# Causal attention with dot-product and geometric logits: scores and maxima as pairs of 64-row tiles, masks in VectorE, both V blocks of a step in a row

## The reference, cut to what matters

```
q, k, v     = split(x @ qkv_w + qkv_b)                     # 16 heads x 16
dot_logits  = (q @ k.T) * 16 ** -0.5
w, r        = exterior(x_prev @ w1_write, x @ w2_write), exterior(x @ w1_read, x @ w2_read)   # 16 heads x 6, unit length
geo_logits  = (r @ (w @ J6).T) * inc_scale                 # x_prev: the token before
combined    = (1 - gate) * softmax(causal(dot_logits)) @ v + gate * softmax(causal(geo_logits)) @ geo_v
y           = layernorm(x + combined @ out_w + out_b)
out         = layernorm(y + (silu(y @ wg.T) * (y @ wu.T)) @ wd.T)
```

## Time and profile before

| | us |
|---|---|
| median of 3 runs (2104.53 to 2110.35) | 2105.75 |
| profiled execution, from its first to its last instruction | 2112.1 |
| TensorE / ScalarE / VectorE / GpSimd busy in it | 1930.6 / 1273.4 / 1129.4 / 336.9 |
| `project`, until the first score | 0 to 251 |
| `attend` | 251 to 1766 |
| `finish` | 1766 to 2112 |

### The profile page before, as it was taken

How to read it: one execution, slowest core, us unless ns; L and a number is a source line. 1 busy time by engine, 2 the same in 40 slices (tenths; PEclk the granted TensorE clock), 3 DMA queues, 4 the chain that set the end, 5 groups by cost and what they waited for, 6 DMA issues and landing times. The chain is left out here.

```text
span 2112.1 us, 35917 instructions
## 1 busy us (share of the span) xinstructions
PE 1930.6 (91%) x11400; PEld 769.0 (36%) x11400; DVE 1129.4 (53%) x2179; ACT 1273.4 (60%) x1641; POOL 336.9 (16%) x609
## 2 busy tenths in 40 slices
PE   8888498999998999999899999989999995899998
PEld 4444122333332333333233333323333322556555
DVE  5666377565564655556465655646565403443442
ACT  4555544577776777677677767767777783222121
POOL 3333303111211110111111011111101111000000
PEclk9999699999999999999999999999999997999999
DMA  6668660404133250414324041432500004112000
GB/s 192 205 211 254 163 107 25 86 21 90 37 70 46 50 86 6 91 20 73 49 47 86 6 91 21 72 46 50 86 6 30 4 11 103 43 51 65 20 20 20
DMA packets 138525, 145.83 MB, mean 69 GB/s; under 512 B 46784, under 2 KB 120768, under 8 KB 136288
## 3 DMA queue, kind: packets, MB, share of 16 engines
q1 hardware_dynamic: 137136, 140.32, 30.4%
q0 software_dynamic: 624, 2.75, 0.4%
q10 hardware_dynamic: 576, 0.28, 0.1%
HBM read 88.25 MB, written 54.53 MB: 68 GB/s over the span
## 5 line engine op out<-in xcount | busy, mean ns | idle before, releaser
L931 ACT ACTIVATE prob<-ex 128x1024 f32<-128x1024 f32 (+2 forms) x1280 | 1074.5, 893 | 444.4 <-PE ex L776 438.8
L946 DVE TENSOR_REDUCE mp<-mx 128x1 f32<-128x512 f32 (+3 forms) x1280 | 749.2, 609 | 547.4 <-PE mx L794 287.5
L776 PE MATMUL ex<-qa,ka 98*128 98x512 bf16 (+3 forms) x2560 | 675.6, 354 | 62.7 <-issue 28.3
L827 PE MATMUL pv<-prob,va 128*32 128x512 f32 (+3 forms) x5120 | 613.4, 552 | 7.6 <-POOL prob L752 7.3
L791 PE MATMUL mx<-ka,qa 96*128 96x512 bf16 (+3 forms) x1280 | 450.1, 353 | 14.7 <-DVE mp L946 13.8
L752 POOL TENSOR_SCALAR_AFFINE_SELECT prob<-prob 128x256 f32<-128x256 f32 x512 | 205.8, 408 | 1288.3 <-ACT prob L931 1287.8
L776 PEld LDWEIGHTS ex<-qa,ka 98*128 98x128 bf16 x2560 | 200.2, 99 | 474.3 <-ACT prob L931 306.3
L791 PEld LDWEIGHTS mx<-ka,qa 96*128 96x128 bf16 x1280 | 123.7, 97 | 340.4 <-DVE mp L946 239.1
L827 PEld LDWEIGHTS pv<-prob,va 128*32 128x32 f32 x5120 | 101.7, 108 | 206.7 <-issue 181.8
L1291 ACT ACTIVATE sg<-pg 128x512 f32<-128x512 f32 x48 | 28.7, 597 | 185.6 <-PE pg L1213 185.5
L794 PE MATMUL mx<-mask_qk,ident 128*128 128x128 bf16 x512 | 113.1, 221 | 0.0
(11 more groups left out here) (101 smaller groups left out, 964.7 us busy)
## 6 DMA issues: line engine op xcount, KB each, us to landing
parts<-sp SPq DMA_DIRECT2D x64, 384.0 KB, 3.3
qa<-parts SPq DMA_DIRECT2D x192, 128.0 KB, 6.7
ka<-parts SPq DMA_DIRECT2D x192, 128.0 KB, 8.6
values<-vn SPq DMA_DIRECT2D x64, 256.0 KB, 3.3
va<-values SPq DMA_DIRECT2D x16, 1024.0 KB, 13.8
heads<-on SPq DMA_DIRECT2D x64, 128.0 KB, 1.9
att<-heads SPq DMA_DIRECT2D x64, 128.0 KB, 3.0
xc<-in_xt SPq DMA_DIRECT2D x8, 513.0 KB, 4.2
```

The source lines that it names most:

```text
L776: last = pe.matmul(dst, ka[which][0:NROWM, h, kb * P:(kb + 1) * P], qa[which][0:NROWM, h, (qt + 1) * CH - w:(qt + 1) * CH], start=True, st ...
L827: last = pe.matmul(pv[h * VW:(h + 1) * VW, qt % 2, CH - w:CH], va[kind][:, kb, h * VW:(h + 1) * VW], prob[(s * HG + h) % 8][:, at[j]:at[j] ...
L931: act.activation(prob[n % 8][:, 0:w], ex[:, n % 2, 0:w], ACT.Exp).then_inc(ex_done, 1)
L946: v.tensor_reduce(out=mp[kind][:, h * NKB + qb, k0 // CH:k0 // CH + 1], in_=mx[:, u % 2, 0:w], axis=AX.X, op=ALU.max).then_inc(mx_free[kin ...
```

## The change

A unit of a step is now one block of two heads, each head's scores in one bank of the slot: units 0 and 1 are the first block, 2 and 3 the second. For GEO, 6 components in 6 products and 2 maxima rows are 38 rows; the two heads of a unit stand on partitions 0 to 37 and 64 to 101. A DOT score matmul reads 98 or 128 partitions and stays one per head and block. The maxima of DOT use the four larger products only (64 rows), and two heads stand on partitions 0 to 63 and 64 to 127: a tile is now a pair of heads in both banks of `mx`, 80 for a pair p, and it waits for the tile right before it. The mask matmul is gone; VectorE adds the mask in float32 and takes the maximum in one operation for each head on the diagonal, while off the diagonal one operation reads both banks.

TensorE's order in a step is: unit 0, 1, 2, 3, then V block 0 and V block 1 of the step before; maxima stand before unit 0, after unit 1, after unit 3 and after the V blocks. The maxima are spread anew, 28 to the DOT item and 52 to the GEO item of a pair. By steps 0 to 17 they are 2 1 1 3 1 1 2 1 2 2 1 1 2 1 2 2 1 2 in DOT, 3 1 4 3 3 1 4 3 3 4 3 1 3 3 4 3 3 3 in GEO, and 7 5 2 6 6 6 5 6 2 6 6 6 6 6 5 in steps 3 to 17 of the first item.

`project` has six groups of rows in place of eight (16 heads by 6 components are 96 rows), each with its own t and d. The maxima rows reach `qa` by four DMAs. Memsets on GpSimd prepare the rows around the operands.

```diff
-Q_PARTS = [0, 0, 1, 1, 0, 2]
-K_PARTS = [0, 1, 0, 1, 2, 0]
-NROW = DH * len(Q_PARTS)
-NROWM = NROW + 2
+Q_SLOTS = (1, 0, 2)
+K_SLOTS = (1, 2, 0)
+FIRST_SLOT = ((0, 1), (1, 0))
+DOT_MAIN = 4 * DH
+GEO_ROWS = 6 * NCOMP
+GEO_FULL = GEO_ROWS + 2
+HALF = 64
+DOT_FULL = (6 * DH + 2, P)
+DOT_AT = ((0, 64), (64, 0))
+DOT_MAX_AT = (96, 32)
...
-NEX = NSTEP * HG
+UNITS = 4
+NEX = NSTEP * UNITS
...
-    for h in range(HG):
+    for pair in range(HG // 2):
         for qb in range(NKB):
             end = (qb + 1) * P
             for k0 in range(0, end, CH):
-                out.append((h, qb, k0, min(CH, end - k0), k0 + CH >= end))
+                out.append((pair, qb, k0, min(CH, end - k0), k0 + CH >= end))
...
-def spread(steps_of):
-
+def spread(room):
+
+    cost = [(2 * w + 300) if d else (2 * w + 150) for _, _, _, w, d in MAXT]
...
-WHERE = [(), (5,), (1, 4), (1, 3, 5), (0, 1, 3, 5), (0, 1, 3, 4, 5), (0, 1, 2, 3, 4, 5)]
+def room(share, first=0):
+
+    return [share * sum(w for _, w in STEPS[s][1]) if first <= s < MT_STEP else 0 for s in range(NSTEP)]
+
+
+GEO_SHARE = 1.9
+_TWO = spread(room(1.0) + room(GEO_SHARE))
 MAX_IN_DOT, MAX_IN_GEO = _TWO[:NSTEP], _TWO[NSTEP:]
+MAX_IN_FIRST = spread(room(1.0, 3))
+
+
+WHERE = [(), (1,), (1, 2), (0, 1, 2), (0, 1, 2, 3)]
...
-    NR = 8
+    NR = 6
+    SLOTS = [Q_SLOTS, Q_SLOTS, K_SLOTS, K_SLOTS, Q_SLOTS, K_SLOTS]
+    ROWS = [P, P, P, P, H * NCOMP, H * NCOMP]
...
-        ln = sb("ln", [P, TT, 2, H, DH])
-        t32 = [sb(f"t32_{i}", [P, CH]) for i in range(4)]
-        d32 = [sb(f"d32_{i}", [P, CH]) for i in range(4)]
+        ln = sb("ln", [P, TT, 2, H, NCOMP])
+        t32 = [sb(f"t32_{i}", [P, CH]) for i in range(NR)]
+        d32 = [sb(f"d32_{i}", [P, CH]) for i in range(NR)]
...
+            for a in range(2):
+                g.memset(first["k"][HALF * a + 32:HALF * a + 64, :, :], 1.0).then_inc(ones_in, 1)
+            g.wait_ge(ones_in, 2)
...
-                        src = ln[:, tt, (m - 4) // 2, (m % 2) * 8:(m % 2) * 8 + 8, :]
-                        last = pe.transpose(pr[m % 4][:, tt * P:(tt + 1) * P],
+                        src = ln[:, tt, m - 4, :, :]
+                        last = pe.transpose(pr[m % 4][0:ROWS[m], tt * P:(tt + 1) * P],
                                             src.rearrange("p h d -> p (h d)"), ident[:, :])
...
+                act.activation(sp3[m][0:n, SLOTS[m][0], :], pr[m % 4][0:n, :], ACT.Identity, bias=bias,
+                               scale=scale).then_inc(row_act, 1)
 
             def second_part(c, m):
                 act.wait_ge(d_done, c * NR + m + 1)
-                act.activation(sp3[m][:, 1, :], d32[m % 4][:, :], ACT.Copy).then_inc(p2_done, 1)
+                n = ROWS[m]
+                act.activation(sp3[m][0:n, SLOTS[m][1], :], d32[m][0:n, :], ACT.Copy).then_inc(p2_done, 1)
...
-                for i in range(2):
-                    q.dma_start(qa[which][NROW + i:NROW + i + 1, :, :].rearrange("p h (k t) -> p (h k) t", t=P),
-                                mrow[:, i, :]).then_inc(m_in, 16)
+                n = HG // 2 * NKB
+                for a in range(2):
+                    for i in range(2):
+                        if which == 0:
+                            at = HALF * a + GEO_ROWS + i
+                            dst = qa[0][at:at + 1, :, :]
+                        else:
+                            at = DOT_MAX_AT[a] + i
+                            dst = qa[which][at:at + 1, 2 * a:2 * a + 2, :]
+                        q.dma_start(dst.rearrange("p h (k t) -> p (h k) t", t=P),
+                                    mrow[a * n:(a + 1) * n, i, :]).then_inc(m_in, 16)
...
+        dull = sb("dull", [P, 2, CH])
...
+                if it < 2:
+                    i = it + 1
+                    done = 3 + it * 4
+
+                    g.wait_ge(masked, (it * len(DIAGONAL) + len(DIAGONAL) - TT // 2) * UNITS)
+                    g.memset(ka[i][96:98, 0:2, :], 1.0).then_inc(ones_ready, 1)
+                    g.wait_ge(ones_ready, done + 1)
+                    g.memset(ka[i][32:64, 2:4, :], 0.0).then_inc(ones_ready, 1)
+                    g.wait_ge(ones_ready, done + 2)
+                    g.memset(qa[i][32:64, 2:4, :], 0.0).then_inc(ones_ready, 1)
+                    g.wait_ge(ones_ready, done + 3)
+                    g.memset(ka[i][32:34, 2:4, :], 1.0).then_inc(ones_ready, 1)
+                    g.wait_ge(ones_ready, done + 4)
...
-                at, _ = place(s)
-                for (kb, w), c0 in zip(blocks, at):
-                    dst = ex[:, slot, c0:c0 + w]
-                    last = pe.matmul(dst, ka[which][0:NROWM, h, kb * P:(kb + 1) * P],
-                                     qa[which][0:NROWM, h, (qt + 1) * CH - w:(qt + 1) * CH],
+                kb, w = blocks[u // 2]
+                for a in range(2):
+                    dst = ex[:, pair, a * CH:a * CH + w]
+                    if kind == GEO:
+                        rows, at = slice(HALF * a, HALF * a + GEO_FULL), pair
+                    else:
+                        rows, at = slice(0, DOT_FULL[a]), 2 * a + pair
+                    last = pe.matmul(dst, ka[which][rows, at, kb * P:(kb + 1) * P],
+                                     qa[which][rows, at, (qt + 1) * CH - w:(qt + 1) * CH],
                                      start=True, stop=True)
                 last.then_inc(ex_ready, 1)
 
             def max_tile(p, kind, which, use, u):
 
-                h, qb, k0, w, on_diagonal = MAXT[u]
-                if qb == 0 and h % 2 == 0:
-
-                    pe.wait_ge(qk_in[which][h // 2], use * 12 * 16)
-                if u >= 2:
-
-                    pe.wait_ge(mx_free[kind], p * (NMX * COUNT[kind]) + (u - 1) * COUNT[kind])
-                dst = mx[:, u % 2, 0:w]
-                last = pe.matmul(dst, qa[which][0:NROW, h, qb * P:(qb + 1) * P],
-                                 ka[which][0:NROW, h, k0:k0 + w], start=True, stop=not on_diagonal)
-                if on_diagonal:
-                    last = pe.matmul(dst[:, w - P:w], ident16[:, :], mask_qk[:, :], start=False, stop=True)
+                pair, qb, k0, w, _ = MAXT[u]
+                if qb == 0:
+
+                    pe.wait_ge(qk_in[which][pair], use * 12 * 16)
+                if u >= 1:
+
+                    pe.wait_ge(mx_free[kind], p * (NMX * COUNT[kind]) + u * COUNT[kind])
+                for a in range(2):
+                    n = GEO_ROWS if kind == GEO else DOT_MAIN
+                    rows, at = slice(HALF * a, HALF * a + n), pair if kind == GEO else 2 * a + pair
+                    last = pe.matmul(mx[:, a, 0:w], qa[which][rows, at, qb * P:(qb + 1) * P],
+                                     ka[which][rows, at, k0:k0 + w], start=True, stop=True)
                 last.then_inc(mx_ready[kind], COUNT[kind])
...
-                at, _ = place(s)
+                if s in DIAGONAL:
+
+                    pe.wait_ge(masked, (it * len(DIAGONAL) + DIAGONAL.index(s)) * UNITS + 2 * j + 2)
+                else:
+
+                    pe.wait_ge(ex_done, it * NEX + s * UNITS + 2 * j + 2)
                 if j == 0:
-                    if s in DIAGONAL:
-
-                        pe.wait_ge(masked, (it * len(DIAGONAL) + DIAGONAL.index(s) + 1) * HG)
-                    else:
-
-                        pe.wait_ge(ex_done, it * NEX + s * HG + HG)
...
                 for h in range(HG):
+                    a = h % 2
                     last = pe.matmul(pv[h * VW:(h + 1) * VW, qt % 2, CH - w:CH],
                                      va[kind][:, kb, h * VW:(h + 1) * VW],
-                                     prob[(s * HG + h) % 8][:, at[j]:at[j] + w],
+                                     prob[(s * UNITS + 2 * j + h // 2) % 8][:, a * CH:a * CH + w],
                                      start=kb == 0, stop=end, tile_position=(0, h * VW))
-                if j == 1:
-                    last.then_inc(pv_step, 1)
+                last.then_inc(pv_half, 1)
...
-                where = [WHERE[min(len(later), 6)].count(i) for i in range(6)]
-                where[5] += max(len(later) - 6, 0)
+                where = [WHERE[min(len(later), 4)].count(i) for i in range(4)]
+                where[3] += max(len(later) - 4, 0)
...
-                scores(it, which, s, 0, head)
                 some(0)
-                scores(it, which, s, 1, head)
+                scores(it, kind, which, s, 0, head)
+                scores(it, kind, which, s, 1, head)
                 some(1)
+                scores(it, kind, which, s, 2, head)
+                scores(it, kind, which, s, 3, head)
+                some(2)
                 if has_before:
                     times_v(*before, 0, head)
-                some(2)
-                scores(it, which, s, 2, head)
+                    times_v(*before, 1, head)
                 some(3)
-                scores(it, which, s, 3, head)
-                some(4)
-                if has_before:
-                    times_v(*before, 1, head)
```

(30 more changed lines are left out.)

146 lines of the change are left out of this document (71 added, 75 removed).

## The result

The changed kernel takes 2555.5 us (median of 4 runs, 2553.4 to 2562.1) against 2108.05 of the kernel before on the same chip: 1.213 times as long, interval 1.210 to 1.215. The forecast was 2282, its range 2160 to 2400.

The account below looks back on a forecast made before the run. It took a chain of scores, V blocks and exps beside TensorE's columns as the bound, with VectorE late in GEO. -24 + 12 + 7 x 17.9 + 7 x 7.3 + 12.4 = +176.8 on 2112.1, less 6.3: 2282 us, range 2160 to 2400.

Parts of the forecast that it names:

- V blocks in a row: Both V blocks behind unit 3: chain of a full DOT step without maxima 5.06 us, replacing 4.87.
- A DOT item and the last one: Later DOT items 101.0 us each, +7.3; the last item, without maxima, 93.9, taken as +12.4.
- Maxima as pairs: Maxima tiles filling both banks: VectorE reads 1024 columns in 1.22 us, pairs come 1.70 apart, masking operation 0.69.
- The two halves at once: GEO score matmuls in different array halves: if they run at once, a unit is 0.22 us, latency 0.43.
- no-overlap rival: Pairs do not overlap on TensorE, each costing 0.21 us more on the chain: +122, 2404 us; chance 0.11.
- `project`: Its ring of dependent work per chunk, 27.37 us, starts 3.07 earlier with two d fewer; together -24 us.
- the forecast's own sign of being wrong: Sign for `project`: no exp-independent ring of a chunk longer than 24.3 us.
- Smaller operand DMAs ... cost or give nothing: none of them is waited for now.: Operand loads, in the same breath as GpSimd's memsets and V waits by halves: no cost or gain.
- GEO item 108 and first item 155: Items slowed by maxima pairs waiting for VectorE: GEO 108.2 us, +17.9 each; first item 155, +12.
- The clock: Rival: TensorE's granted clock falls to 0.78 in new GEO steps, +90, 2372 us; chance 0.12.
- TensorE's columns: Rival: columns streamed by TensorE set the time, so fewer columns make it faster, 1906 us; chance 0.05.
- cheap reading: Rival: VectorE reads a pair in the time of one tile, maxima 1.17 apart, 2167 us; chance 0.08.

Follow-up runs that it names:

- e1_loads: Changed kernel with operand DMAs taken head row by head row, outermost dimension 6 or 16 instead of 2: 2455.2 us.
- e14_rows64: e1_loads with GEO score matmuls over 64 rows of each half instead of 38: 2378.7 us.
- e4_before_vrow: Kernel before, with only V block 0 moved right before V block 1, behind the four scores: 2248.1 us.
- e2_loads_vsplit: e1_loads with V block 0 put back between the second and third score unit of a step: 2206.5 us.
- e11_vrow_again: e2_loads_vsplit plus banks handed over singly and maxima 40 to 40, then V blocks in a row again: 2344.8 us.

## Why the prediction was wrong, step by step

- **V blocks in a row: right at 2.4 GHz.** 5.06 was forecast for a full step without maxima. The last item of the changed kernel has 5.12, with a gap of 1.35 (ScalarE):

```profile
2189.35 3.77 ACT L968 ACTIVATE prob<-ex 128x1024 f32<-128x1024 f32 x4 [1.35 <-PE ex L815]
2194.47 3.77 ACT L968 ACTIVATE prob<-ex 128x1024 f32<-128x1024 f32 x4 [1.35 <-PE ex L815]
```

- **A DOT item and the last one: right**, +6.1 for +7.3 and +15.0 for +12.4; the last item takes 93.9 from its first exp to its end, as forecast.
- **Maxima as pairs: prices right at 2.4 GHz** (1.225 for 1.22, 0.688 for 0.69, VectorE by form, 400 to 2150 us). The fetch of each result, 0.083, lies beside the next operation. Two pairs with nothing between them are 1.71 apart, for the 1.70 of the forecast, where the clock is 1.00 (the first two lines of the second view), and 1.94 where it is 0.5 (the last two), for which the forecast had no term:

```profile
L993 DVE TENSOR_REDUCE mp<-mx 128x2 f32<-128x1024 f32 x346 | 424.0, 1225 | 432.6 <-PE mx L832 431.4
L989 DVE CUSTOM_DVE_ANT_0 dull<-mx,mask_qk 128x512 f32<-128x512 f32 x114 | 74.2, 688 | 52.7 <-PE mx L832 52.7
...
L989 DVE DVE_READ_ACCUMULATOR2_ANT mp<- 128x1 f32 x456 | 37.8, 83 | 0.0
```

```profile
794.94 1.23 DVE L993 TENSOR_REDUCE mp<-mx 128x2 f32<-128x1024 f32 x1 [0.49 <-PE mx L832]
796.65 1.23 DVE L993 TENSOR_REDUCE mp<-mx 128x2 f32<-128x1024 f32 x1 [0.49 <-PE mx L832]
...
304.75 1.23 DVE L993 TENSOR_REDUCE mp<-mx 128x2 f32<-128x1024 f32 x1 [0.71 <-PE mx L832]
306.69 1.23 DVE L993 TENSOR_REDUCE mp<-mx 128x2 f32<-128x1024 f32 x1 [0.71 <-PE mx L832]
```

- **The two halves at once: right.** The four 38-row score matmuls at 1076.50 above take 0.60; four 98-row ones take 1.04 at the same clock (1195.56, timeline of a DOT item):

```profile
1195.56 1.04 PE L815 MATMUL ex<-qa,ka 98*128 98x512 bf16 x4
```

  The no-overlap rival is out.
- **`project`: nearly right.** Chunks without operand loads give a ring of 22.5 to 23.5 (forecast at most 24.3), two of them below. The chunk in which SyncE issues the GEO operands takes 30.7, over the forecast's own sign of being wrong (25.6 in e1_loads):

```profile
115.66 0.21 DVE L550 TENSOR_TENSOR gate_z<-gz,bg 128x64 f32 x1
138.26 0.21 DVE L550 TENSOR_TENSOR gate_z<-gz,bg 128x64 f32 x1
161.50 0.21 DVE L550 TENSOR_TENSOR gate_z<-gz,bg 128x64 f32 x1
192.19 0.22 DVE L550 TENSOR_TENSOR gate_z<-gz,bg 128x64 f32 x1
```

- **First failed step: "Smaller operand DMAs ... cost or give nothing: none of them is waited for now."** The DOT ones were not smaller, 128 KB each as before, and with outermost dimension 2 they took 2.1 us to issue where the kernel before, with 16, took 0.37 (first line below, before). The one who waited was mostly not a reader of the operands but the reader of a store behind them on the same queue. Undoing it gave 100 of the 272 us. In the first item it also showed at once: TensorE stood 19.4 us for `ka` (second line).

```profile
L179 SPq DMA_DIRECT2D qa<-parts x192: 316/372/1655, 174.7 to 1507.9; - x192
```

```profile
261.79 0.29 PE L832 MATMUL mx<-ka,qa 64*128 64x128 bf16 x2 [19.42 <-DMA ka<-parts_dot]
```

- **Second failed step: GEO item 108 and first item 155, both reckoned at 2.4 GHz.** The clock stood among the rivals with 0.12, and even there at 0.78 and +90; it was 0.73 and 0.61. What is left after e1_loads, 21 in each of seven GEO items and 36 in the first, goes with it: GEO items of e1_loads and e14_rows64, which differ in rows alone, take for instance 141.8, 133.4, 127.3 and 119.6 at 0.70, 0.77, 0.84 and 0.90. A straight line through all fourteen is 113 at 0.96, the clock of GEO items before (no item lies more than 3 us off it); the forecast is 95.6 + 17.9 = 113.5 by the same marks. That is an extrapolation: no run had the changed order of a GEO item at that clock. The price of the clock was reckoned too low for two reasons. The forecast spread a mean of 0.78 over the 2.8 us of TensorE's work in a step, but the low level falls on the longest piece of the chain: both V blocks in a row take 3.4 to 3.6 there for the forecast's 1.84, at a clock of 0.54 in a step of the changed kernel:

```profile
1089.20:1092.50 3.30, 3.30 (x18) 0.56 (x16) 1.23 (x1) 0.35 (x1) 0.00 (x0) 0.54 0.00 0
```

  And the pairs of maxima come 0.23 later each, as above. So the order of V was right by itself (+140 on the kernel before, e4_before_vrow) and dearer beside a clock that falls with it (249 between e1_loads and e2_loads_vsplit, 254 in e11_vrow_again).
- **The other rivals.** TensorE's columns (1906) and cheap reading (2167) are out: ScalarE's busy share fell to 48%, TensorE's to 77%, and 1024 columns took 1.225.

What stays open: how the clock is decided. No single thing explains the low clock of GEO items. Each of four edits raised its mean there from e1_loads's 0.75: rows in use (38 to 64 rows, 0.87), more score matmuls (0.87), V blocks apart (0.87), shorter waits for maxima (0.79). None of them brought it back alone; with 64 rows in both halves, V apart, banks handed over singly and 40 pairs it was 0.91 to 0.98, close to the 0.95 to 0.98 before.
